# Metaformer block with a routed expert layer: the last chunk's routing placed between the first expert tiles, the second set's padding stored behind eight loads, a reordered opening, and ten row and result buffers

## What is computed

```python
x = x + relu(conv3x3_groups8(layernorm_c(x)) + bias)       # x: 16 x 16 x 16 x 128
t = tokens(x)                                              # 4096 tokens of 128
n = layernorm(t)
logits = n @ router_w.T                                    # 8 experts
w, e = top_k(logits, 2); w = softmax(w)
t = t + sum_k w_k * (silu(n @ w_gate[e_k]) * (n @ w_up[e_k])) @ w_down[e_k]   # 128 -> 256 -> 128
```

## Time and profile before

| | us |
|---|---|
| median of 3 runs | 252.48 |
| lowest and highest run | 252.00, 255.03 |
| profiled execution | 252.54 |
| its span from the first to the last instruction | 250.8 |
| TensorE busy | 201.3 (80%) |
| VectorE busy | 156.6 (62%) |
| ScalarE busy | 126.1 (50%) |
| GpSimd busy | 151.5 (60%) |
| mean granted clock of TensorE | 0.917 of 2.4 GHz |

### The profile page before, as it was taken

The page is one execution under the profiler, slowest core; times in us unless marked ns, Lnnn a source line. Parts: engine busy times, 40 slices in busy tenths (PEclk is TensorE's granted clock), DMA queues, the critical chain, the costliest instruction groups (busy, mean ns, idle before and its releaser), DMA issues.

```text
span 250.8 us, 4798 instructions
## 1 busy us (share of the span) xinstructions
PE 201.3 (80%) x1214; PEld 171.1 (68%) x1214; DVE 156.6 (62%) x628; ACT 126.1 (50%) x332; POOL 151.5 (60%) x184
## 2 busy tenths in 40 slices
PE   7997996996979536699699999589999999995000
PEld 7685784874868425588598888488887888884000
DVE  2568769989978982755355555535698666563044
ACT  2545976785677414255345665426555555563000
POOL 7342373677777777777777665626565667666400
PEclk9999999997999965799889999979999999999555
DMA  5999011111432551111334334241594333621194
GB/s 150 357 372 345 4 54 33 48 50 47 117 80 74 125 135 52 50 50 55 92 88 106 89 79 121 72 111 42 147 316 102 83 88 89 192 85 38 35 319 148
DMA packets 32922, 29.09 MB, mean 116 GB/s; under 512 B 5093, under 2 KB 26729, under 8 KB 32896
## 3 DMA queue, kind: packets, MB, share of 16 engines
q1 hardware_dynamic: 27920, 20.08, 28.5%
q0 software_dynamic: 4544, 8.50, 10.3%
q10 hardware_dynamic: 432, 0.20, 0.3%
HBM read 16.97 MB, written 12.71 MB: 118 GB/s over the span
## 4 chain that ended last, share of the span: by engine, by line
PE 35%; DVE 21%; DMA 11%; POOL 10%; issue 9%; SPq 7%; ACT 5%; POOLq 1%; DVEq 0%; ACTq 0%
PE ps_y L463 8%; POOL zs L991 7%; DMA yb<-y,zt 4%; PE ps_gu L439 4%; PE ps_h L451 4%; PE ps_gu L441 4%; PE ps_gu L440 4%; PE ps_gu L356 3%; DMA zt<-zs 3%; DMA spare<-yb 2%; ACT xn L541 2%; POOL yb L999 2%; PE ps_z L428 2%; SPq L310 2%; PE ps_y L336 2%
## 5 line engine op out<-in xcount | busy, mean ns | idle before, releaser
L999 POOL DMA_INDIRECT yb<-y,zt x78 | 76.3, 979 | 42.6 <-ACT y L613 27.3
L991 POOL DMA_INDIRECT zs<-rows,slot x64 | 62.9, 982 | 26.1 <-issue 21.8
L869 DVE SCALAR_TENSOR_TENSOR hh<-ps_gu,zt,sg 128x256 f32<-128x256 f32 x78 | 34.2, 479 | 43.6 <-ACT sg L604 43.6
L604 ACT ACTIVATE sg<-ps_gu,zt 128x256 f32<-128x256 f32 x78 | 32.9, 471 | 34.1 <-PE ps_gu L441 34.0
L356 PE MATMUL ps_gu<-pad,ckw 128*128 128x256 f32 x192 | 45.1, 384 | 0.1
L463 PE MATMUL ps_y<-wall,hT 128*128 x312 | 42.8, 282 | 0.0
L356 PEld LDWEIGHTS ps_gu<-pad,ckw 128*128 128x128 f32 x192 | 36.0, 192 | 7.9 <-issue 3.2
L463 PEld LDWEIGHTS ps_y<-wall,hT 128*128 128x128 f32 x312 | 39.5, 199 | 0.1
L439 PE MATMUL ps_gu<-wall,z_lo 128*128 x78 | 36.0, 462 | 0.0
L613 ACT ACTIVATE y<-ps_y,zt 128x128 f32<-128x128 f32 x78 | 24.4, 365 | 22.6 <-PE ps_y L463 22.6
L440 PE MATMUL ps_gu<-wall,z_hi 128*128 x78 | 32.0, 410 | 0.0
(11 more groups left out here) (125 smaller groups left out, 239.4 us busy)
## 6 DMA issues: line engine op xcount, KB each, us to landing
zt<-zs SPq DMA_DIRECT2D x78, 65.5 KB
spare<-yb SPq DMA_DIRECT2D x16, 256.0 KB, 4.3
rows<-x_rows SPq DMA_DIRECT2D x8, 256.0 KB, 6.2
spare<-gate_up_w SPq DMA_DIRECT2D x8, 256.0 KB, 6.2
xc<-x_cols SPq DMA_DIRECT2D x8, 256.0 KB, 6.3
out<-rows SPq DMA_DIRECT2D x8, 256.0 KB, 3.4
yb<-y,zt POOLq DMA_INDIRECT x78, 2.4
zs<-nulls SPq DMA_DIRECT2D x18, 65.5 KB, 3.6
```

The costliest lines, as they stand in the source:

```text
L604: last = nc.scalar.activation(sg[u % 2][:, s, :], ps_gu[u % 2][:, s * N:s * N + H], ACT.Silu, scale=zt[:, u % RING, s, RSTD:RSTD + 1])
L869: last = nc.vector.scalar_tensor_tensor(hh[u % 2][:, s, :], ps_gu[u % 2][:, s * N + H:(s + 1) * N], zt[:, u % RING, s, RSTD:RSTD + 1], sg[ ...
L991: nc.gpsimd.indirect_dma_start(zs[g], bass.IndirectOffsetOnAxis(slot[:, k, n * TT + t:n * TT + t + 1], 0), rows[:, k, n * TT + t, :], None ...
L999: nc.gpsimd.indirect_dma_start(yb, bass.IndirectOffsetOnAxis(zt[:, u % RING, s, ID:ID + 1].bitcast(U32), 0), y[u % YB][:, s, :], None, bou ...
```

## The change

RING (the ring of loaded rows) and YB (the result buffers) go from 8 to 10. On SyncE pad_regions loses its last waits, which become regions_filled; the null rows of set 1 are stored between the loads of unit 7 and unit 8, and only regions_filled(1) stands ahead of unit 20. On TensorE, ScalarE and VectorE transpose_z(0), z_heads(0) and z_tails(0) move ahead of parts of chunk 7's routing: logits and transpose_t of chunk 7 follow transpose_z(0), its rank follows gate_up(0); its statistics follow gated(0), its slots gated(1), table(1) gated(2), and table_row(1) opens iteration 3. In the opening, chunk 0 is normalised ahead of the first weight, the keep_warm products are placed anew (12, 4 and 4 become 10 and 6), weights 1 to 3 move later, and the statistics of chunks 4 and 5 with their root (group 3) stand together ahead of residual(1).

```diff
--- before.py
+++ after.py
@@ -59,8 +59,8 @@
 ROW = P + 3
 ID, WEIGHT, RSTD = P, P + 1, P + 2
 WROW = 2 * 2 * H + 2 * P
-RING = 8
-YB = 8
+RING = 10
+YB = 10
 NOWHERE = 1 << 20
 PIECE = 4
 MAGIC = 1597463007.0
@@ -273,6 +273,8 @@
                     skip_runtime_bounds_check_because="a region's count is at most the tokens of the set")
                 for e in range(E):
                     sp.dma_start(zs[g][bass.ds(ends_at[e], P), :], nulls[:]).then_inc(nulls_stored[g], 16)
+
+            def regions_filled(g):
                 for n in range(*SET_CHUNKS[g]):
                     sp.wait_ge(scattered[n], 16 * 2 * TT)
                 sp.wait_ge(nulls_stored[g], 16 * (E + 1))
@@ -319,8 +321,11 @@
                                  ).then_inc(out_stored, 16)
 
             pad_regions(0)
-            load_set(0, FIRST[1])
+            regions_filled(0)
+            load_set(0, 8)
             pad_regions(1)
+            load_set(8, FIRST[1])
+            regions_filled(1)
             load_set(FIRST[1], FIRST[1] + 8)
             gather_rows(0)
             load_set(FIRST[1] + 8, UNITS)
@@ -466,21 +471,19 @@
                 last.then_inc(yps_ready, 1)
 
             pe.wait_ge(ident_ready, 1)
-            keep_warm(12)
+            keep_warm(10)
             pe.wait_ge(rw_loaded, 16)
             pe.wait_ge(centre_ready, 2)
             nc.tensor.matmul(ps_h[:, 0:E], centre[:], rwT[:], start=True, stop=True).then_inc(rwT_ready, 1)
+            keep_warm(6)
             centre_weights(0)
+            transpose_x(0)
             centre_weights(1)
-            keep_warm(4)
-            transpose_x(0)
-            keep_warm(4)
             pe.wait_ge(ckw_ready, 1)
             conv(0, 0)
-            centre_weights(2)
             conv(0, 1)
             transpose_x(1)
-            centre_weights(3)
+            centre_weights(2)
             pe.wait_ge(rwc_ready, 1)
             logits(0)
             transpose_t(0)
@@ -492,37 +495,39 @@
                     transpose_t(n - 1)
                 else:
                     rank(0)
+                    centre_weights(3)
                 if n + 1 < CHUNKS:
                     transpose_x(n + 1)
                 conv(n, 1)
+                if EARLY + n - 1 < E:
+                    centre_weights(EARLY + n - 1)
                 if n >= 2:
                     rank(n - 1)
-                if EARLY + n - 1 < E:
-                    centre_weights(EARLY + n - 1)
                 if n == SET_CHUNKS[0][1] + 1:
                     table(0)
+            at = {}
+            pe.wait_ge(pad_even, CHUNKS - 1)
+            pe.wait_ge(pad_odd, CHUNKS - 1)
+            transpose_z(0)
             logits(CHUNKS - 1)
             transpose_t(CHUNKS - 1)
-            rank(LAST)
-
-            at = {}
-            pe.wait_ge(pad_even, CHUNKS)
-            pe.wait_ge(pad_odd, CHUNKS)
             pe.wait_ge(relu_ready, CH * CHUNKS)
-            pe.wait_ge(t_copied, 2 * CHUNKS)
             pe.wait_ge(w_hi_ready, E)
             pe.wait_ge(w_lo_ready, E)
             pe.wait_ge(down_loaded, 16)
-            transpose_z(0)
             for u in range(UNITS + 2):
                 if u < UNITS and (u - FIRST[SET_OF_UNIT[u]]) % 4 == 0:
                     at.update(experts_of(u, min(u + 4, FIRST[SET_OF_UNIT[u]] + SLOTS[SET_OF_UNIT[u]])))
+                if u == 3:
+                    table(1)
                 if u + 1 < UNITS:
                     transpose_z(u + 1)
+                if u == 1:
+                    pe.wait_ge(t_copied, 2 * CHUNKS)
                 if u < UNITS:
                     gate_up(u, at[u])
-                if u == 1:
-                    table(1)
+                if u == 0:
+                    rank(LAST)
                 if 1 <= u <= UNITS:
                     transpose_h(u - 1)
                 if u >= 2:
@@ -619,18 +624,17 @@
             act.dma_start(rwT[:], router).then_inc(rw_loaded, 16)
             act.wait_ge(neghalf_ready, 3)
             nc.scalar.activation(th[:], neghalf[:, 0:BT], ACT.Silu)
+            normalise_x(0)
             weight_heads(0)
-            normalise_x(0)
-            weight_heads(1)
             act.wait_ge(pads_zeroed, 2)
             pads(0)
+            weight_heads(1)
             normalise_x(1)
             act.wait_ge(bias_loaded, 16)
             conv_relu(0, 0)
-            weight_heads(2)
             conv_relu(0, 1)
             pads(1)
-            weight_heads(3)
+            weight_heads(2)
             copy_rows(0)
             normalise_x(2)
             for n in range(1, CHUNKS):
@@ -640,6 +644,7 @@
                 if n + 1 < CHUNKS:
                     pads(n + 1)
                 if n == 1:
+                    weight_heads(3)
                     row_scalars(0)
                 conv_relu(n, 1)
                 if n + 2 < CHUNKS:
@@ -648,14 +653,15 @@
                     weight_heads(EARLY + n - 1)
                 if n >= 2:
                     row_scalars(n - 1)
+            z_heads(0)
             copy_rows(CHUNKS - 1)
-            row_scalars(CHUNKS - 1)
-            z_heads(0)
             for u in range(UNITS + 2):
                 if u + 1 < UNITS:
                     z_heads(u + 1)
                 if u < UNITS:
                     silu(u)
+                if u == 1:
+                    row_scalars(LAST)
                 if u >= 2:
                     y_rows(u - 2)
 
@@ -899,31 +905,34 @@
                 ck[:].rearrange("p k (g o) -> p k g o", g=1).broadcast_to([P, CH * BANDS * 2, HG, GC]),
                 own[:].rearrange("p (k g) o -> p k g o", k=1).broadcast_to([P, CH * BANDS * 2, HG, GC]),
                 ALU.mult).then_inc(ckw_ready, 1)
-            weight_tails(0)
             dve.wait_ge(pads_zeroed, 2)
             pad_odds(0)
             stats_x(1)
             variance_x(1)
+            weight_tails(0)
             dve.wait_ge(rwT_ready, 1)
             nc.vector.tensor_copy(rwc[:], ps_h[:, 0:E]).then_inc(rwc_ready, 1)
-            weight_tails(1)
             shift_x(1)
             stats_x(2)
-            weight_tails(2)
+            weight_tails(1)
             stats_x(3)
             variance_x(2)
             pad_odds(1)
             dve.wait_ge(iod_ready, 6 + len(SETS))
             residual(0)
             shift_x(2)
+            weight_tails(2)
             top_two(0)
             stats_t(0)
             deviation_t(0)
-            weight_tails(3)
             slots(0)
             scale_gap(0)
             pass_on(0)
+            weight_tails(3)
             stats_x(4)
+            stats_x(5)
+            variance_x(3)
+            shift_x(3)
             for n in range(1, CHUNKS):
                 residual(n)
                 if n >= 2:
@@ -932,30 +941,37 @@
                         pass_on(n - 1)
                 if EARLY + n - 1 < E:
                     weight_tails(EARLY + n - 1)
-                if n <= 3:
-                    stats_x(n + 4)
-                if n in (1, 3):
-                    variance_x(n // 2 + 3)
-                    shift_x(n // 2 + 3)
+                if n in (1, 2):
+                    stats_x(n + 5)
+                if n == 3:
+                    variance_x(4)
+                    shift_x(4)
                 if n == SET_CHUNKS[0][1]:
                     table(0)
                 if n == SET_CHUNKS[0][1] + 1:
                     table_row(0)
+                if n == CHUNKS - 1:
+                    z_tails(0)
                 top_two(n)
-                stats_t(n)
-                deviation_t(n)
-                scale_gap(n)
-            slots(LAST)
-            z_tails(0)
+                if n < CHUNKS - 1:
+                    stats_t(n)
+                    deviation_t(n)
+                    scale_gap(n)
             for u in range(UNITS + 2):
+                if u == 3:
+                    table_row(1)
                 if u + 1 < UNITS:
                     z_tails(u + 1)
                 if u < UNITS:
                     gated(u)
                 if u == 0:
+                    stats_t(CHUNKS - 1)
+                    deviation_t(LAST)
+                    scale_gap(LAST)
+                if u == 1:
+                    slots(LAST)
+                if u == 2:
                     table(1)
-                if u == 1:
-                    table_row(1)
                 if 1 <= u <= UNITS:
                     h_cols(u - 1)
                 if 0 <= u - FIRST[1] - 4 < NT[0] // PIECE:
```

## The result

| | before | after |
|---|---|---|
| median of the runs, us | 252.6 (252.0 to 255.03, 4 runs) | 238.36 (237.39 to 243.25, 4 runs) |
| ratio, 95% interval | | 0.9446 [0.9388, 0.9504] |
| profiled execution / its span | 252.54 / 250.8 | 238.63 / 236.9 |

The change saves 14.2 us, 5.5%. In some sets a run or two come out some 2% longer, the ratios leave these out, and the profiled execution of after_again (243.75) is one of them.

The account below looks back on a forecast made before the run. GpSimd's unbroken run of dispatches and stores was taken to bound the kernel through the gather releasing unit 28. Unit 28 moves from 188.83 to 179.3, so 252.5 - 9.5 = 243.0 us, range 239.7 to 247.0.

Parts of the forecast that it names:

- Run start 42.6: GpSimd's dispatches from chunk 1 on: the unbroken run starts at 42.6 instead of 44.59, 2.0 us earlier.
- Null stores at 101 to 107: SyncE's padding of set 1: starts after the second table, about 101, and takes 5.7 us, hidden before unit 8.
- Unit 5's transposes 106.2: TensorE's first units: 87.1 + 15.2 + 3.9 for VectorE's last-chunk work gives 106.2, against 111.23 before.
- my 41.9: VectorE's opening: slots(1) end at 41.9, 9.1 us after residual(1) at 32.8; GpSimd's run starts 0.6 later.
- the time from the 39th store to the gather: End of set 0: store ends 164.0, then 0.3, a 3.35 us landing and 0.3 more put the gather at 168.0.
- my unit 28 (179.3): TensorE's transposes of unit 28: 178.4 from the gather plus 0.9 for the clock, against 188.83 before.
- rival E: Whole kernel: the change only moves the wait, 247.4 us and up, gain at unit 28 shrunk to 5.1; chance 0.10.
- The stall that did not come: VectorE waits 5.9 us for the first gathered piece, TensorE idles some 5 us, and its fallen clock adds 0.9.
- 23 x 2.95 - 1.5 = 66.4 us: TensorE alone from unit 5 to unit 28, at 2.95 us a unit: it would reach unit 28 at 172.5.
- the rival with all small terms good: Whole kernel: run 3.3 us earlier, store 2.24, stall short; unit 28 at 176.0, total 239.7; chance 0.10.
- rival A: Opening: VectorE's longer block leaves GpSimd no gain or costs it a us; total 245.0 to 246.2; chance 0.15.
- the second wait: TensorE's 3.35 us before unit 20, ascribed to padding issued behind all loads of set 0; moving the padding removes it.

Follow-up runs that it names:

- after_again: The changed kernel unaltered, in a second set of runs where before took 251.94 us: 241.39 us, ratio 0.9547.
- a_padold: The changed kernel with the null rows of set 1 stored behind the load of unit 19 again: 244.86 us, ratio 0.9770.
- a_all_2: The changed kernel with residual(1) earlier, unit 2's tails first, the gather behind unit 31's loads and rings of 12: 233.98 us, ratio 0.9259.
- a_resid_2: The changed kernel with VectorE's residual(1) ahead of three statistics, chunk 6's behind chunk 1's: 238.88 us, ratio 0.9457.

## Why the prediction fell short

**Right.** The bound was read rightly: GpSimd's run of dispatches and stores, the gather behind it, unit 28, then 62 us as before. Run start 42.6, measured 41.78. First store 114.5, measured 113.28. Residual(0) 18.3, measured 17.43. Units 8 and 20 wait for nothing. Null stores at 101 to 107, measured 98.73 to 102.71; they came sooner, since SyncE waits there for the region ends and not, as I wrote, for the whole table. Gather to unit 28 10.4, measured 10.68.

**Right by luck.** Unit 5's transposes 106.2, measured 106.10: unit 1 came 1.7 us sooner than forecast (85.43 against 87.1), and the way from unit 1 to unit 5, with the waits for which I had charged 3.9, took 1.6 more. The start of the run was near for another reason than mine: slots(1) were ready 1.6 us before my 41.9, but the dispatch waited for ScalarE's row_scalars(1), which my sum doesn't have.

**The step that failed most: the time from the 39th store to the gather.** I wrote "114.5 + 38 x 1.277 = 163.1, end 164.0. Then 0.3, a store of 3.35, the gather's issue 0.3 later at 168.0". GpSimd's timeline of before shows the error:

```profile
172.76 0.97 POOL L999 DMA_INDIRECT yb<-y,zt  x1 [0.30 <-issue]
174.04 0.97 POOL L999 DMA_INDIRECT yb<-y,zt  x1 [0.30 <-issue]
```

The DMA of 3.35 us in the earlier trace rows starts at 172.76, with its own instruction, not behind it; so 0.97 + 0.3 was counted twice. And the two rows are the 37th and 38th store, not, as I wrote, the 39th, which is the one at 174.04. In after the 39th store starts at 161.78, its DMA record runs from 161.78 for 2.40, and the gather is issued at 164.27: 2.49 us behind the store's start, where my sum has 4.9. Of the 2.4 us too much, 1.27 are the instruction counted twice, 0.95 the store (3.35 against 2.40), and 0.2 the step from its landing to the issue. These 2.4 us are the larger part of the 4.35 us between my unit 28 (179.3) and the measured 174.95. The run gives 1.3 more (0.8 by its start, the rest by 71.5 us instead of 71.9 and 48.5 instead of 48.6), the stall below 0.9, and the gather's way to unit 28 takes 0.3 back. With the 39th store at 174.04 in before, the pauses in my rival E were 9.0 us and not 6.4. The Trainium skill (Perfetto Trace Analysis, Summary: the profiler window per engine type) says that the instruction's record of a GpSimd DMA ends with its descriptors and hides the data's movement; the trace agrees, 0.97 us beside 2.40 from one start. The Trainium skill's figure for the fixed part of such a DMA, which the prediction named as saying 1.2 us less (DMA: Bandwidth & Descriptors, Anatomy of one DMA), was the nearer one here.

**The stall that did not come.** I added 0.9 us for a clock that falls behind 5 us of idle TensorE, as VectorE would wait for the first gathered piece at 172.7. VectorE's timeline of after, its first addition:

```profile
169.20 0.69 DVE L892 TENSOR_TENSOR rows<-rows,spare 128x512 f32<-128x512 f32 x1
```

The 4.7 us of the earlier trace rows weren't a landing time: VectorE came to that addition without a wait, so the piece was there by then at the latest. In after it waits for nothing either: with the gather 3.7 us earlier the piece is there at about 169.0 (an estimate: 164.27 and 4.7, the median from issue to landing of these loads in after), and VectorE comes to it at 169.2 instead of 166.8. The second half of that is an error of its own. I had counted 23 x 2.95 - 1.5 = 66.4 us for TensorE from unit 5 to unit 28; they took 68.9, of which only 0.63 is the wait before unit 28, since some units take more than 2.95 us (3.28 from unit 16 to 17; 3.32 in before). TensorE alone would have reached unit 28 at 174.3 and not at 172.5. So the two bounds lay 0.6 us apart, where by my own terms the gather's was nearly 6 us behind TensorE's.

**The range.** Its low end, 239.7, was the rival with all small terms good: run earlier, store short, no stall, and these came true or nearly (2.8 us earlier instead of 3.3, 2.40 instead of 2.24). It still held the instruction counted twice, 1.27 us, and 239.7 - 1.27 = 238.4. A range whose cases share one wrong term is too narrow by that term. Nor did I give a case to the clock behind the 1.92 us of idle TensorE that my own count produced (residual(1) later than before, "rival A"). The largest spread seen between executions of the kernel goes with it: the 241.39 us of the second set lie inside my range, with a D1 of 47.14 in its profile. That a median of 241 would have been inside is no merit of the sum, which has no such term.

**What the parts are worth.** By the table: the ring 8.4 us alone, the opening 2.8 (D1 44.59 to 41.78), the padding 2.7 more (197.8 to 195.1), the last chunk 0; together 13.9, the difference of the spans. The padding's 2.7 are what is left over when the others are taken off; taken back by itself it was 3.2. The opening's 2.8 hold for the good execution only. I had ascribed the second wait to the padding alone. The experiment in the kernel before shows that the two buffers remove that as well; the padding's 2.7 us come on top, where TensorE reaches unit 20 sooner (a_padold waits 2.52 us for it at 156.18).

## What to carry to other kernels

When one engine issues in an unbroken run, write every later event as its start plus a constant, and look for what starts the run; here 195 to 196 us behind D1 held over six executions of five kernels, while taking away a wait of 3 us of TensorE moved nothing. A DMA record that starts with its instruction already contains it, so take the pair's start and add once; and check that all cases of a range don't share such a term. Where two engines are nearly balanced at the end, try both bounds in one edit: TensorE's alone gave nothing, both together 4.9 us (GpSimd's alone wasn't run).

## What the runs showed of the hardware

- An idle time of 1.92 us on TensorE was followed by a granted clock of 0.57 to 0.74 in the window of 34 to 38 us in six profiled executions and of 1.00 in one, with the same instructions around it; in the four executions of the 290 us condition that have it, by 0.50 to 0.57. In the four executions with residual(1) moved, which don't have it, the clock of that window is 1.00. Another idle time, of 1.68 us before logits(2), was followed by 0.50 in 42 to 44 us in a_all_2 and by 1.00 in a_resid_2. The Trainium skill (TensorE: Matmul & The Clock Gate, Why this matters for your kernels) tells of longer gaps; the traces show that these can be enough, and need not be. The price was 2.1 us on one conv and 1.7 to 3.3 on D1.
- GpSimd's indirect stores of 128 rows go out every 1.28 us, 0.97 busy and 0.30 between, dispatch and result store alike, 95 in a row in after (56 and 39); the data of one land 2.4 us behind its start (median; 2.24 to 3.35 in the rows shown).
- A chip can be in a condition in which the same kernel takes 290 instead of 252 us, with gaps of up to 15.6 us whose cause the trace doesn't name, and an edit worth 14 us is worth nothing there (ratio 1.0061 [1.0006, 1.0116]).
